# The tail of each batch row in an eight-row AdaLN kernel: another order for its last products, and other DMAs for the next row's query and key parts

## The reference

```python
h = _layernorm(x) * (1 + ca) + sa
x = x + ga * _L0_attn_ref(h, ...)      # causal softmax attention, 16 heads of 8
h = _layernorm(x) * (1 + cb) + sb
x = x + gb * _L0_ffn_ref(h, ...)       # 8 experts, top 2
h = _layernorm(x) * (1 + ca) + sa      # second layer, its own modulation
x = x + ga * _L1_attn_ref(h, ...)      # gated delta net, 12 heads, state 64 x 128
h = _layernorm(x) * (1 + cb) + sb
x = x + gb * _L1_ffn_ref(h, ...)       # gelu feed-forward, scaled by a router
```

```python
var = jnp.mean(o * o, axis=-1, keepdims=True)
o = o * jax.lax.rsqrt(var + 1e-05) * g_norm_weight
o = o * g * jax.nn.sigmoid(g)
return o.reshape(b, l, VD) @ Wo
```

## Time and profile before

| | |
|---|---|
| median of 3 runs | 2632.04 us |
| lowest, highest | 2618.61, 2632.81 us |
| the profiled execution | 2622.98 us, span 2621.3 us |
| granted TensorE clock, mean | 0.984 |
| busy: PE, DVE, ACT, POOL | 90%, 65%, 53%, 32% |
| the chain that ended last, by engine | PE 57%, ACT 17%, DVE 8%, DMA 6%, SP's queue 3% |

### The profile page before, as it was taken

One profiled execution on the slowest core, in us unless ns is written; L12 is line 12 of the kernel. 1 busy time (PEld: TensorE's weight loads), 2 busy tenths in 40 slices (PEclk: granted clock), 3 DMA queues, 4 the chain that ended last, 5 costly groups with the idle time before them and its releaser, 6 DMA issues.

```text
span 2621.3 us, 63954 instructions
## 1 busy us (share of the span) xinstructions
PE 2350.2 (90%) x23763; PEld 1625.5 (62%) x23763; DVE 1694.2 (65%) x4218; ACT 1397.1 (53%) x3001; POOL 845.0 (32%) x589
## 2 busy tenths in 40 slices
PE   3899988999898998989979899898988999889998
PEld 2456865568554776548745587455774567655685
DVE  2557764677637777377764776557764677656776
ACT  0466444764447554485543855447444574446644
POOL 3136121452205422064301642125321262213621
PEclk8999999999999999999999999999999999999999
DMA  8301132011310103101130012301132011320113
GB/s 261 119 1 21 19 102 83 4 20 17 111 74 4 26 11 110 74 9 21 29 130 37 13 20 64 123 5 19 19 104 83 1 20 19 103 83 1 23 17 106
DMA packets 226953, 137.98 MB, mean 53 GB/s; under 512 B 173567, under 2 KB 209799, under 8 KB 219431
## 3 DMA queue, kind: packets, MB, share of 16 engines
q1 hardware_dynamic: 208870, 125.48, 16.8%
q10 hardware_dynamic: 17780, 8.39, 1.1%
HBM read 95.10 MB, written 38.71 MB: 51 GB/s over the span
## 4 chain that ended last, share of the span: by engine, by line
PE 57%; ACT 17%; DVE 8%; issue 7%; DMA 6%; SPq 3%; POOL 1%; ACTq 1%; DVEq 0%; POOLq 0%
PE bank L947 9%; PE bank L717 4%; PE bank L522 4%; PE bank L708 3%; PE bank L639 3%; PE bank L1050 3%; ACT arena L1702 3%; ACT arena L1703 3%; PE bank L842 2%; DVE mx L1214 2%; ACT vq L1710 2%; PE bank L619 2%; PE bank L562 2%; PE bank L971 2%; PE bank L1071 2%
## 5 line engine op out<-in xcount | busy, mean ns | idle before, releaser
L1350 DVE SCALAR_TENSOR_TENSOR arena<-bank,conv,arena 128x510 f32<-128x510 f32 x320 | 237.1, 747 | 44.8 <-ACT arena L1703 26.8
L1998 POOL TENSOR_TENSOR arena<-upto,gk 128x1536 f32<-128x1536 f32 x32 | 88.1, 2753 | 452.9 <-DVE beta L1343 452.9
L1214 DVE TENSOR_REDUCE mx<-bank 128x2 f32<-128x768 f32 (+3 forms) x187 | 201.3, 1123 | 46.8 <-PE bank L563 45.6
L1990 POOL TENSOR_TENSOR arena<-arena 128x511 f32<-128x511 f32 x160 | 201.8, 1272 | 56.0 <-DVE arena L1350 56.0
L522 PE MATMUL bank<-mask_k,ident_bf 128*128 128x512 bf16 x824 | 211.2, 388 | 0.0
L1666 ACT ACTIVATE arena<-bank 128x384 f32<-128x384 f32 (+1 forms) x384 | 168.6, 547 | 46.9 <-PE bank L624 46.8
L779 PE MATMUL bank<-h_pad,arena 128*128 128x512 f32 x320 | 165.6, 615 | 28.5 <-DVE arena L1350 21.7
L562 PE MATMUL bank<-vq 128*128 128x512 bf16 (+3 forms) x544 | 121.2, 308 | 49.1 <-issue 21.4
L1687 ACT ACTIVATE arena<-bank,b1e 128x512 f32<-128x512 f32 x128 | 87.8, 686 | 116.8 <-PE bank L708 111.7
L1316 DVE SCALAR_TENSOR_TENSOR xs<-bank,comb,xs 128x128 f32<-128x128 f32 x256 | 72.1, 344 | 114.8 <-PE bank L717 114.2
L717 PEld LDWEIGHTS bank<-arena 128*128 128x128 f32 x1024 | 122.5, 192 | 23.1 <-issue 22.9
(11 more groups left out here) (307 smaller groups left out, 5784.7 us busy)
## 6 DMA issues: line engine op xcount, KB each, us to landing
vq<-q_rows SPq DMA_DIRECT2D x18, 1024.0 KB, 7.9
vq<-k_rows SPq DMA_DIRECT2D x18, 1024.0 KB, 10.9
arena<-w_bounce SPq DMA_DIRECT2D x16, 1024.0 KB, 6.0
q_rows<-qkp SPq DMA_DIRECT2D x81, 128.0 KB, 2.4
k_rows<-qkp SPq DMA_DIRECT2D x81, 128.0 KB, 2.4
arena<-wv_rows SPq DMA_DIRECT2D x8, 768.0 KB, 10.2
ogt<-wv_rows SPq DMA_DIRECT2D x8, 768.0 KB, 11.6
t_bounce<-blk_tx SPq DMA_DIRECT2D x32, 192.0 KB, 2.1
```

The costliest lines, as they stand in the source:

```text
L1214: V.reduce_max(dst, unit_scores(u), AX.X).then_inc(s_max, 1)
L1350: ins = V.scalar_tensor_tensor(a[:, k:T], ps[:, 0:T - k], conv[:, n, 3 - k:4 - k], a[:, k:T], ALU.mult, ALU.add)
L1990: G.tensor_tensor(acc[:, n % 4, 1:T], acc[:, n % 4, 1:T], second(n)[:, 0:T - 1], ALU.add).then_inc(taps_added, 1)
```

## The change

- The three parts of `q` and of `k` are written to HBM once each, to new arrays `q_parts` and `k_parts` (6 DMAs of 128 KB in place of 18). The stacks are loaded in more pieces: the spare rows (56 partitions) alone, ahead of the parts; the queries' part rows 24 partitions at a time, from a source that is repeated three times (`to_broadcast`); the keys' 72 part rows in one DMA per half, from a source of 24 rows repeated three times. `stacks_in` counts 96 in place of 32.
- On PE, `project` of chunks 2 and 3 waits for each group of four heads by itself. Chunk 3 is turned and projected in the order of groups 2, 0, 1.
- For chunk 3, L1493 and L1495 stand ahead of `outputs`. DVE multiplies group 2 of `ob` by its gate (one 128x512 instruction) while ACT works on the factor. ACT then scales the four heads of group 2 (four instructions), DVE the eight others.
- `row_max` of the first score unit stands between `normalise` and `modulate` of the row's last layer norm, no longer behind it.

The core of the diff: PE's `project`, DVE's `square`, ACT's new `scale`, SP's new loads.

```diff
 def project(c, lot=range(HD)):
     ps = wo_bank(c)
+    if c + 2 >= NT:
+        for i, g in enumerate(turned(c)):
+            pe.wait_ge(ogt_ready, at(b, ogt_ready, NG * c + i + 1))
+            for j in range(GH):
+                h = GH * g + j
+                last = mm(ps[:, 0:D], ogt[:, h, :], wo[:, h, :], start=(i + j == 0), stop=(i == NG - 1 and j == GH - 1))
...
+        def turned(c):
+            return (2, 0, 1) if c + 1 == NT else (0, 1, 2)
...
 def square(c):
...
-    query_factor(c)
+    V.tensor_tensor(fac[:, 0, :], fac[:, 0, :], fac[:, 2, :], ALU.mult).then_inc(ot_ready, 1)
+    dve.wait_ge(gate_ready, at(b, gate_ready, NG * NT))
+    V.tensor_tensor(ob[:, HS[2], :], ob[:, HS[2], :], gate(c)[:, HS[2], :], ALU.mult).then_inc(dve_step, 1)
...
+def scale(c):
+    if c + 1 < NT:
+        return
+    act.wait_ge(of_made, at(b, of_made, 1))
+    for h in range(HD)[HS[2]]:
+        ins = A.mul(og[:, h, :], ob[:, h, :], fac[:, 1, h:h + 1])
+    ins.then_inc(on_scaled, 1)
...
+def load_spare(half):
+    hs = heads_of(half)
+    for stack, source in zip((q_stack, k_stack), stack_rows):
+        sp.dma_start(stack[KS:P, hs, :], source[KS:P, hs, :]).then_inc(stacks_in[half], 16)
+def load_queries(half, n):
+    hs, rows = heads_of(half), PARTS * DA
+    sp.dma_start(q_stack[rows * n:rows * (n + 1), hs, :],
+                 q_parts[n, :, hs, :].unsqueeze(0).to_broadcast([PARTS, DA, HA // 2, T])).then_inc(stacks_in[half], 16)
+def load_keys(half):
+    hs = heads_of(half)
+    every = k_parts.rearrange("n d h t -> (n d) h t")[:, hs, :]
+    sp.dma_start(k_stack[0:KS, hs, :], every.unsqueeze(0).to_broadcast([PARTS, PARTS * DA, HA // 2, T])).then_inc(stacks_in[half], 16)
```

More of the change, by code:

```diff
@@ L258, in adaln_two_layers @@
         idx = sb("idx", [P, NT, 8], U32)
+        part_rows = [dram(n, [PARTS, DA, HA, T], BF16) for n in ("q_parts", "k_parts")]
         stack_rows = [dram(n, [P, HA, T], BF16) for n in ("q_rows", "k_rows")]
@@ L1547, in _ @@
                     p2 = small[:, 104:112].rearrange("p (c i) -> p c i", c=NT)
-                    row_max(b, 1, 0)
                     row_max(b, 1, 1)
@@ L2071, in enter_parts, with write, heads_of @@
             def enter_parts(b, ahead):
[L2073 to L2079, removed]
+                q_parts, k_parts = part_rows
+                def write(i, n):
+                    sp.wait_ge(qk_parts, at(b, qk_parts, PARTS * i + n + 1, ahead))
+                    sp.dma_start(part_rows[i][n].rearrange("d h t -> h d t"), qkp[:, i, n, :]).then_inc(parts_out[i], 16)
+                def heads_of(half):
+                    return slice(HA // 2 * half, HA // 2 * (half + 1))
+                def load_spare(half):
[10 more added lines that the diff above has]
+                    sp.dma_start(k_stack[0:KS, hs, :], every.unsqueeze(0).to_broadcast([PARTS, PARTS * DA, HA // 2, T])).then_inc(stacks_in[half], 16)
+                for n in range(PARTS):
+                    write(0, n)
                 if ahead:
@@ L2082, in enter_parts @@
                     sp.wait_ge(qs_ps, at(b, qs_ps, NG * NT))
-                for i in range(2):
-                    for stack, source, out in zip((q_stack, k_stack), stack_rows, parts_out):
-                        if i == 0:
-                            sp.wait_ge(out, at(b, out, IN_ROW[out.name], ahead))
-                        hs = slice(8 * i, 8 * i + 8)
-                        sp.dma_start(stack[:, hs, :], source[:, hs, :]).then_inc(stacks_in[i], 16)
+                load_spare(0)
+                write(1, 0)
+                sp.wait_ge(parts_out[0], at(b, parts_out[0], IN_ROW[parts_out[0].name], ahead))
+                for n in range(PARTS):
+                    load_queries(0, n)
+                write(1, 1)
+                load_spare(1)
+                write(1, 2)
+                for n in range(PARTS):
+                    load_queries(1, n)
+                sp.wait_ge(parts_out[1], at(b, parts_out[1], IN_ROW[parts_out[1].name], ahead))
+                load_keys(0)
+                load_keys(1)
             def maxima(b, ahead, i):
```

48 lines of the change are left out of this document (32 added, 16 removed).

## The result

The changed kernel takes 2798.15 us (median of 4 runs) beside 2625.32 us for the kernel before on the same chip: ratio **1.065, 95% interval 1.0592 to 1.0709**, slower. The profiled execution took 2804.54 us, 181.6 more than the one of before, where 129 were forecast.

What follows compares the result with a forecast made beforehand. The landing of the low keys, which PE's scores await, was taken as the bound. Eight rows of 12.4 + 1.6 us plus 17 us ahead of the loop made 129 us on 2622.98: 2752, median put at 2755, range 2695 to 2800.

Steps and rivals of the forecast that it cites:

- The landing of the low keys decides: End of each row: PE's first score waits for the low keys' load; the other path has about 0.9 us to spare.
- Three engines for the repeated loads: Query and key loads run on 3 of 16 DMA engines, one per copy; 12.4 us a row lost, chance 0.83.
- 0.31 us for a packet of the spare rows: DMA queue ahead of the last key write: 8-KB packets at 0.31 us of one engine, 2.5 us per spare lot.
- 1.6 us a row for the lower clock: PE resuming after about 17 us idle runs at the lower clock, costing 1.6 us a row (0 to 3).
- Ahead of the loop 17 us: The same DMAs run once before the loop, sharing engines with ACT's weights: 17 us later, 8 to 25 as ends.
- The bodies: Rest of each row, from the turn of the maxima to POOL's next part; the forecast's sum has no term for it.
- `row_max` 1.05 us: DVE, last norm of a row: the moved maximum hides in idle time, so the router's L1552 comes 1.05 us sooner.
- Writes once: SP's queue of key-part writes: twelve writes of 128 KB, 1.8 us to be won at the last key write's issue.
- The earlier end of the projection: Last projection and `xn` at a row's end: about 2.5 us earlier, worth zero by itself, having room to spare.
- all 16 engines: Rival: all engines carry the new loads; low keys land 2.1 us sooner, 3.15 us a row won, 2598 us; chance 0.11.
- nothing moves at the landing: Rival: pieces spread well but queued loads eat the 1.8 us; only `row_max` pays, 2615 us; chance 0.03.
- only the keys or only the queries: Rival: only one kind of load is confined to three engines; keys alone 2 to 4 us late, 2640 to 2665; chance 0.03.

Runs made afterwards that it cites:

- e2_new_loads: The kernel before with only the change's DMAs (parts written once, repeated-source loads, spare rows alone): 2805.1 us, ratio 1.0654.
- e1_old_loads: The changed kernel with the writes and loads of before, all other edits kept: 2637.46 us, ratio 1.0017.
- e12_row_order: The changed kernel with the 72 rows reordered so the repeat stands inside, same number of transfers: 2664.68 us, ratio 1.0137.
- e4_half_partitions: The kernel before with each load of a stack half split at partition 64, nothing repeated: 2674.87 us, ratio 1.0173.
- e14_low_first: The changed kernel with the high half's spare rows and queries issued behind the low keys: 2727.72 us, ratio 1.0385.
- e8_row_max: The kernel before with the earlier `row_max` alone: 2616.17 us, ratio 0.9968.
- e6_warm: The changed kernel with 92 more filling matmuls behind the projection, to fill PE's gap ahead of the scores: 2792.87 us, ratio 1.0625.
- e10_warm: e1_old_loads with 12 more filling matmuls behind the projection: 2621.54 us, ratio 0.9988 to the kernel before.
- e9_projection: e1_old_loads without the earlier `row_max`, so the projection edits alone on the loads of before: 2632.48 us, ratio 1.0034 to the kernel before.
- e13_row_order_low_first: e12_row_order with the high half's spare rows and queries issued behind the low keys: 2632.5 us, ratio 1.0017 to the kernel before.

## Why the prediction was right, and where it fell short

The forecast was 2755, with 2695 to 2800 as its range, and 2798 was measured: slower, by the mechanism named. That it lies inside the range is in part luck. It is 2 us from the end, less than the runs differ among themselves, and 13 above the mechanism's own range of 2719 to 2785. (That range takes its lower end from the profiled execution and its upper end from the median; from the profiled one alone its terms give 2719 to 2776, and the profiled execution after took 2804.54.) By the steps of the prediction:

- **The landing of the low keys decides:** shown. The whole loss comes with `e2_new_loads`, and the first score stands where it stood in `e1_old_loads`, though the projection ends sooner.
- **Three engines for the repeated loads:** shown. The share is 0.19, and the keys' load took 14.90 us, worked out as 15.1 (told at 2608.3, issued at 2593.2; 1.5 of these, until a landing is told, stand in no row). With the repeat inside it takes 6.44. The Trainium skill ("DMA: Bandwidth & Descriptors", "Rules for kernel authors") names this cause, a leading broadcast of few copies. `e12_row_order` agrees, since the same repeat further in runs at a share of 0.67.
- **0.31 us for a packet of the spare rows: the step that failed.** It was carried over from loads of 128 partitions to loads of 56. They took about twice that: the window of 188 GB/s at a share of 0.91, with 0.63 us in the median for its packets of 8 KB, and 0.62 in `e4_half_partitions`. Two lots of 4 + 4 packets stand ahead of the last key write, sized at 2.5 us each; at 0.64 they are some 5.1, 5 us more in all. The last write lands at an offset of 26.8 where 22.2 was forecast, 4.6 later, and the first score comes 17.5 us later than before in place of 13.5. That is 32 of the missing 52 us.
- **1.6 us a row for the lower clock:** 2.0 measured, 3 us in all.
- **Ahead of the loop 17 us:** 23, inside its ends of 8 and 25. Most of it is the repeat's place too: the first score there stands at an offset of 34.2 before, 57.3 in the changed kernel, 46.2 in `e14_low_first` and 38.9 in `e12_row_order`.
- **The bodies** were taken as unchanged and took 12 us more. The seven between the loop's tails sum to 1904 us before, to 1914 in the changed kernel and in `e2_new_loads` alike, but to 1895 in `e8_row_max` and 1923 in `e6_warm`. They go with the time that the clock spent at its lower level in them: 38, 58, 55, 17 and 75 us in this order, and their sum is longer by about half of what that time is. `e10_warm` has 58 us too, with the loads of before, so the loads need not be the reason; what starts the dips stays open.
- **`row_max` 1.05 us:** shown by `e8_row_max`, 8 us over eight rows.
- **Writes once:** the last key write starts 1.3 us sooner against POOL's first part, forecast 1.8; worth nothing here. (The row read as 0.6 us for the issue of a write says 0.52; nine in a row took 6.51 us in that tail, 0.72 each.)
- **The earlier end of the projection:** 2.2 us of the forecast 2.5 are there, though the product with the sums (L1526), forecast at 0.17 us, took 0.64; it ran beside POOL's last part and ended with it, at 2744.90 and 2744.88. "Worth by itself: zero" was wrong for this part alone: it costs 9 us (`e9_projection`). The wait that it lengthens is PE's, and in six of eight tails the clock falls in it or just behind it. In the changed kernel it doesn't show, PE being idle for 20 us anyway.
- **The rivals:** "all 16 engines" fell with the share of 0.19; "nothing moves at the landing" and "only the keys or only the queries" fell with the 17.5 us.

## What to carry to other kernels

Before loads are cut into pieces, count for each piece the engines that it gets and the rate at which its partitions can take it. Then add all that stands in the queue ahead of the write or load on the critical path: fewer bytes or fewer transfers are no measure. A source that is repeated a few times belongs inside the access pattern; outermost, three copies left three engines at work here. And an engine that gets done sooner only to wait longer isn't free where that engine is PE: fill the gap, or leave the work where it was.

## What the runs showed of the hardware

- A load into partitions of one half only, 0 to 63 or 64 to 127, ran at 217 GB/s with all engines busy, 0.62 us for a packet of 8 KB; into all 128 it is 426 GB/s and 0.31 us.
- The same 72-partition load with its source repeated three times landed in 14.90 us with the repeat outermost and in 6.44 us with it inside (unlike queues ahead of them; 12.18 us for the first with the high half's queries and spare rows out of the way). The DMA share was 0.19 and 0.67.
- PE's clock in the first scores: 1.00 behind 1.49 us of idle time and 0.40 us (`e10_warm`); 0.50 behind 3.33 us (`e1_old_loads`). Between them no length of the gap decides. The two tails of `e9_projection` that kept the full clock had the shortest gaps of their kernel, 2.7 us, the six others 3.1 to 3.8; but one tail of `e1_old_loads` kept it with 3.3 us, four of `e13_row_order_low_first` with 2.7 to 3.7, and one of `e6_warm` lost it behind 2.3.
